# Large matmuls dealt out between small ones in attention; an evacuation moved ahead in the feed-forward

## The chip, the cores and the metric

One Trainium2 chip, one of its cores. The metric is the device time of one execution in microseconds; lower is better. Engines: PE (TensorE, matmuls and weight loads), DVE (VectorE), ACT (ScalarE), POOL (GpSimd) and SP, whose queue issues the DMAs.

## The reference

The kernel is one transformer layer on x of shape (2, 4096, 512), in fp32, with adaptive layer norms:

```
mod = silu(c) @ wmod                      # six rows: sa, ca, ga, sb, cb, gb
h   = layernorm(x) * (1 + ca) + sa
x   = x + ga * attention(h)               # RWKV-6, 16 heads of 32
h   = layernorm(x) * (1 + cb) + sb
x   = x + gb * ffn(h)

attention: xxx = h + sx * maa_x           # sx: the token before, minus this one
  m = tanh(xxx @ tm_w1); mix = maa + m @ tm_w2     # five mixes
  xw, xk, xv, xr, xg = h + sx * mix[i]
  r, k, v = xr @ Wr, xk @ Wk, xv @ Wv;  g = silu(xg @ Wg)
  w = exp(-exp(decay + tanh(xw @ td_w1) @ td_w2))
  per token: a = k v';  y = r (state + u a);  state = w state + a
  out = (groupnorm(y) * g) @ Wo
ffn: hh = silu(q(x) @ q(w_gate).T) * (q(x) @ q(w_up).T);  out = q(hh) @ q(w_down).T
  q: blocks of 16 along the last axis, rounded to FP4 (E2M1) values times the block's scale
```

The inner width of the feed-forward is 1408.

## The kernel before

**Order.** Nothing schedules the work at run time. Each engine runs a hand-written list of calls; counters (semaphores) tie the engines together, and `after(engine, signal, chunk, k)` makes an engine wait. An engine executes strictly in its own order, so a wait holds everything behind it.

**Attention** runs over 32 chunks of 128 tokens, both batches together. It is a pipeline over three chunks: body i prepares chunk i (`do_p`: mixes and projections), runs the recurrence of chunk c = i - 1 (`do_w`) and finishes chunk f = i - 2 (`do_f`: the product with Wo and the residual). Bodies 3 to 29 are a hardware loop whose lap holds nine bodies; the others are written out. All three parts are there in bodies 2 to 31.

The recurrence of a chunk is cut into eight steps n = 0 to 7: two batches by four blocks of 32 tokens. The parts of step n are, by engine:
- PE `pe_scores` (L424): products of 32x32 tiles of k and r, four row groups by four head slices, in three sets (L434, L438, L440).
- PE `pe_outer` (L442, matmuls L449): the outer products k v'. Its end signals `score_done`.
- DVE `dve_A` (L908): waits for `score_done`, builds the 32x32 decay-weighted matrix A in eight small instructions (its start is L919, s_tmp L926, masked copies L932) and updates the state (L948). Its end signals `A_done`.
- PE `pe_y` (L452; L464, L467): A times v plus state times r; needs `A_done` of its step. In PE's list y(n - 1) comes in step n. `pe_scores(n)` needs `A_done` of step n - 2.

All these small products are 192 matmul records in a step, each with a weight load. Between them stand the large products of the other chunks, each as a block:
- `pe_g` (L534, matmuls L543), the gate projection, one 128-column part in each of steps 0 to 3: four contraction steps k into the PSUM bank `SMALL`. `act_gu` on ACT reads the bank after parts 1 and 3.
- `pe_td1` (L505, L511) in step 4: the decay's first product, into `SMALL`; ACT's tanh (`u1_done`) reads it.
- `pe_wo` (L548, matmuls L558): the output product of chunk f, batch b, four contraction steps of 512 columns each into `SMALL`: b = 0 as (0, 1) in step 5 and (2, 3) in step 6, b = 1 whole in step 7. The first step of b = 0 needs `u1_done`, the first of b = 1 needs DVE's `dve_out(f, 0)` (L978, instruction L981), which reads the bank.
- `pe_td2` (L518) in step 6: the decay's second product, needs all five mixes; DVE's `dve_ww` (L822, L827) reads it.
- `pe_delta` (L498) at the end of steps 1 to 5, for `dve_mix` (L807; L814, and for the first mix L819). POOL adds hT to the other four mixes (`mixadd`, L764).

After step 7's y(6) come `pe_proj` (L530) for k's first half (needs `dve_ww`), y(7), the transposes `pe_x`, the other projections, `pe_tm1`, and scores(0) of the next chunk. On ACT `act_hT` (L613) turns the transposes into hT, on which DVE's `dve_sx` (L795) waits.

DVE's list in a body (`dve_body`, L983): A(0), z, A(1), mix 0, A(2), mix 1, layer-norm statistics, A(3), mix 2, A(4), mix 3, g, A(5), mix 4, A(6), ww, out(b = 0), A(7), out(b = 1), then the decay products (L836 on), yS (L955), sx (L795) and what follows.

**The feed-forward** runs over 64 tiles of 128 tokens, alternating between the two batches (u = 0, 1). For tile n, PE computes gate and up (L1623) in three column slices of 480, 464 and 464, in that order, for which four PSUM banks in two pairs are used in turn: slice 2 of a tile needs the pair of slice 0, so it waits for `dve_h(n, 0)`. Then PE runs the down product of tile n - 1 (L1632). ACT: sil of slice 0 (L1597), the grid and scales of the next tile's x (L1586, L1447), sil 1, statistics of the tile after (L1571 to L1577), sil 2, the layer norm, and the grid and full scales of h (`act_full`, L1447). DVE, in `dve_body` (L1519): the quantiser for x of tile n + 1 (`divide` and `quantise`, L1411 to L1439), `dve_h` for slices 1 and 2 of tile n (L1502), the quantiser for h of tile n (`dve_hq`, L1504), `dve_h` for slice 0 of tile n + 1, and `dve_out` (L1515) for tile n - 1. In the quantiser L1434 makes the rounded values q16h, and L1437 and L1439 multiply them by the high and low part of the scales, which gives hq; SP then issues two transposing DMAs (L1464, L1467) for the down product, behind them the store of the output and the load of a later tile (xl, L1473).

Of the kernel before, what the change touches and what calls it, by code (L numbers as in the profile page):

```python
# [160 lines left out]
def attention(nc, x1, x, maa_x, maa, tm_w1, tm_w2, decay, td_w1, td_w2, faaaa, Wr, Wk, Wv, Wg, Wo,  # L161
              ln_w, ln_b, c_in, wmod, ident_in, diag_in, pick_in, w_gate, w_up, early, ni=NI):
    with ExitStack() as ctx:
# [260 lines left out]
        def pe_scores(pe, c, n):  # L424
            b, q = divmod(n, Q)
            sc, scm = SC[n % 2], XB[n % 2]
            if n == 0:
                settled_after(pe, mod_done, (der, c), (ru_done, c), (m1_done, c), (k_done, c), (derk, c, 2))
            elif n >= 2:
                settled_after(pe, mod_done, (A_done, c, n - 1))  # L430
            for g in range(G):
                X = (g * B + b) * Q + q
                for d in HEADS:
                    nc.tensor.matmul(sc[d, g * NS:(g + 1) * NS], kvar[d, 0, g, b, 32 * q:32 * q + 32], rcol[d, X, 0:M1], start=True, stop=True)  # L434
            for g in range(G):
# [16 lines left out]
        def pe_y(pe, c, n):  # L452
            b, q = divmod(n, Q)
            if n == 0:
# [5 lines left out]
            for g in range(G):  # L460
# [7 lines left out]
            last.then_inc(y_done.sem, 1)  # L468
# [36 lines left out]
        def pe_td1(pe, i):  # L505
            xf_wait(pe, i, 0)
            after(pe, mf_done, i)
            after(pe, gu_done, i - 1)
            for k in range(G):
                for b in range(B):  # L510
                    last = nc.tensor.matmul(SMALL[HALVES[b], 0:TC], w_td1[:, k, :], xf[:, 0, k, b], start=(k == 0), stop=(k == G - 1))  # L511
            last.then_inc(td1_done.sem, 1)
# [21 lines left out]
        def pe_g(pe, c, g, do_p):  # L534
            if g == 0:
# [6 lines left out]
            for k in range(G):  # L542
                last = nc.tensor.matmul(SMALL[:, (g % 2) * BT:(g % 2 + 1) * BT], w_g[:, k, g * P:(g + 1) * P],  # L543
                                        xf[:, NMIX - 1, k].rearrange("p b t -> p (b t)"), start=(k == 0), stop=(k == G - 1))
            if g % 2:
                last.then_inc(proj_done.sem, 1)
# [15 lines left out]
        def pe_body(pe, i, do_p, do_w, do_f, more, more2):  # L562
            c, f = i - 1, i - 2
            if do_w:
                pe_g(pe, c, 0, do_p)
                pe_outer(pe, c, 0)
            for n in range(1, 8):
                if do_w:
                    pe_scores(pe, c, n)
                    pe_outer(pe, c, n)  # L570
                    if n <= 3:
                        pe_g(pe, c, n, do_p)
                if n == 4 and do_p:
                    pe_td1(pe, i)
                if n == 5 and do_f:
                    pe_wo(pe, f, 0, (0, 1), do_p, do_w)
                if n == 6 and do_f:
                    pe_wo(pe, f, 0, (2, 3), do_p, do_w)
                if n == 6 and do_p:
                    pe_td2(pe, i)  # L580
                if n == 7 and do_f:
                    pe_wo(pe, f, 1, (0, 1, 2, 3), do_p, do_w)
                if do_w:
                    pe_y(pe, c, n - 1)
                if n <= 5 and do_p:
                    pe_delta(pe, i, n - 1)
            if do_p:
                pe_proj(pe, i, 1, lambda h: after(pe, ww_done, i), (0,))
            if do_w:
                pe_y(pe, c, 7)  # L590
# [7 lines left out]
            if do_p:  # L598
                pe_proj(pe, i, 3, lambda h: after(pe, ru_done, i, h + 1))
                pe_scores(pe, i, 0)  # L600
# [382 lines left out]
        def dve_body(dve, i, do_p, do_w, do_f, more, more2):  # L983
            c, f = i - 1, i - 2
            for n in range(8):
# [14 lines left out]
                if n == 6 and do_f:  # L1000
                    dve_out(dve, f, 0)
# [82 lines left out]
def feed_forward(nc, out, x1, w_down, c_in, wmod, ident_in, early, nt=2 * NI):  # L1084
# [7 lines left out]
    with ExitStack() as ctx:  # L1092
# [326 lines left out]
        def quantise(dve, n, w, src, m, q, s, s16, s_done, full, full_done, pw, step, grid_done, dst, high, low, freed):  # L1419
# [14 lines left out]
            link(V.scalar_tensor_tensor(q[:], m, GRID, src, ALU.max, ALU.subtract))  # L1434
            freed()
# [68 lines left out]
        def dve_hq(dve, u, n):  # L1504
# [3 lines left out]
                     lambda: (after(dve, hT_high, n - 1), after(dve, hT_low, n - 1)))  # L1508
# [10 lines left out]
        def dve_body(dve, j, u, n, do_m, do_out, more):  # L1519
# [216 lines left out]
```

## Time and profile before

| | us |
|---|---|
| median of 3 runs | 4145.38 |
| lowest and highest | 4139.29, 4150.52 |
| the profiled execution | 4149.2 |
| its span in the profile | 4147.4 |
| one body of attention shown below | 72.8 |
| two successive feed-forward tiles | 22.06, 22.52 |

The span is the profile's time from the first to the last instruction; what lies around it is 1.8 us. Busy time of an engine is the time in which it had an instruction under way. For each instruction the profile says how long its engine was idle before it and what released it; "issue" means that it waited for nothing the profile shows. PE's matmuls overlap, so a group's time is from the start of the first to the end of the last. A matmul on fp32 data is two records.

### The profile page before, as it was taken

The numbers are of one execution on the slowest core, as the hardware profiler recorded it, in microseconds if no ns is written. First come the engines' busy times: TensorE is split into PE (matmuls) and PEld (weight loads), VectorE is DVE, ScalarE is ACT, GpSimd is POOL, SyncE is SP. The second block draws the span as 40 slices with busy tenths as digits, with TensorE's granted clock in tenths as the row PEclk, the third lists the DMA queues.
The fourth block names the chain that finished last, engine by engine and source line by source line (L and its number), as shares of the span: only waits on it lengthen the run. The fifth ranks groups of instructions, "written<-read, shape, count | busy, mean of one in ns | idle before, by whom it ended". The sixth has DMA issues, their size and how long they took to land. (4 is left out here: it accounts for less than half of the span.)

```text
span 4147.4 us, 151943 instructions
## 1 busy us (share of the span) xinstructions
PE 3600.3 (87%) x64072; PEld 2405.7 (58%) x64072; DVE 3358.0 (81%) x7542; ACT 1735.4 (42%) x3493; POOL 918.9 (22%) x737
## 2 busy tenths in 40 slices
PE   4889899898888888888988984299999999999998
PEld 3777677676676676776776762144444444444443
DVE  4788788887888877788887867878888888888887
ACT  2434444344344343443443412344444444444443
POOL 1122222221222222122221213522222222222221
PEclk7999999999999999999999986599999999999999
DMA  4000010000000000000000012023323323323322
GB/s 118 13 24 29 19 34 18 24 28 19 24 28 20 32 19 24 29 19 24 28 24 29 13 69 75 5 69 77 87 74 82 84 72 86 81 75 86 79 77 73
DMA packets 325485, 195.99 MB, mean 47 GB/s; under 512 B 265152, under 2 KB 265920, under 8 KB 324800
## 3 DMA queue, kind: packets, MB, share of 16 engines
q1 hardware_dynamic: 324800, 186.07, 16.2%
q8 instruction: 525, 8.60, 0.9%
q14 instruction: 160, 1.31, 0.1%
HBM read 89.56 MB, written 33.55 MB: 30 GB/s over the span
## 5 line engine op out<-in xcount | busy, mean ns | idle before, releaser
L932 DVE COPY_PREDICATED Am<-pick,banks 128x64 f32<-128x64 uint8 (+2 forms) x1792 | 461.2, 257 | 127.6 <-DVE Am L932 12.4
L764 POOL TENSOR_TENSOR raw_up<-raw_up,raw_gate 128x1024 f32<-128x1024 f32 x128 | 312.4, 2440 | 1084.9 <-DVE raw_up L814 1084.9
L1623 PE MATMUL fbank<-gT,xqT 128*128 128x464 f16 (+1 forms) x2304 | 491.4, 363 | 68.9 <-DVE h L1502 45.9
L1623 PE MATMUL fbank<-uT,xqT 128*128 128x464 f16 (+1 forms) x2304 | 487.7, 361 | 1.8 <-issue 1.7
L1632 PE MATMUL fbank<-dT,hqT 128*128 128x512 f16 x2112 | 467.8, 380 | 8.0 <-DMA hqT<-hq 8.0
L530 PE MATMUL banks<-raw_up,raw_gate 128*128 128x256 f32 x2048 | 459.0, 383 | 1.8 <-DVE xxx L827 1.8
L530 PEld LDWEIGHTS banks<-raw_up,raw_gate 128*128 128x128 f32 x2048 | 386.7, 191 | 54.2 <-issue 2.1
L1623 PEld LDWEIGHTS fbank<-gT,xqT 128*128 128x128 f16 x2304 | 221.2, 98 | 320.0 <-DVE h L1502 70.7
L1623 PEld LDWEIGHTS fbank<-uT,xqT 128*128 128x128 f16 x2304 | 225.4, 98 | 233.5 <-issue 3.1
L775 POOL TENSOR_TENSOR yrs<-yvar,neg_half 128x32 f32<-128x32 f32 x32 | 174.0, 5437 | 834.3 <-DVE yvar L961 834.3
L1632 PEld LDWEIGHTS fbank<-dT,hqT 128*128 128x128 f16 x2112 | 207.1, 98 | 255.9 <-DMA hqT<-hq 8.5
L558 PE MATMUL banks<-w_o,yn 128*128 128x512 f32 x512 | 275.0, 674 | 20.0 <-DVE yn L972 16.2
L814 DVE SCALAR_TENSOR_TENSOR raw_up<-banks,col_maa,sx 128x256 f32<-128x256 f32 x640 | 265.4, 477 | 29.4 <-PE banks L498 28.5
L543 PE MATMUL banks<-raw_up,w_g 128*128 128x256 f32 x1024 | 268.5, 406 | 19.1 <-issue 18.9
L634 ACT ACTIVATE m_stack<-xxx 32x256 fp32r<-32x256 f32 x512 | 211.9, 414 | 99.4 <-DVE xxx L805 80.9
L440 PE MATMUL banks<-rcol,kvar 32*32 32x16 f32 x8192 | 194.7, 177 | 60.5 <-issue 60.4
L438 PE MATMUL banks<-rcol,kvar 32*32 32x48 f32 x8192 | 204.5, 205 | 41.4 <-issue 41.1
L464 PEld LDWEIGHTS banks<-Am,v_s 32*32 32x32 f32 x8192 | 155.6, 107 | 145.3 <-issue 141.3
L530 PE MATMUL banks<-raw_up,w_v 128*128 128x256 f32 x1024 | 229.5, 382 | 0.0
L665 ACT ACTIVATE xxx<-xxx 128x1024 f32<-128x1024 f32 x32 | 33.8, 1057 | 466.6 <-DVE xxx L827 466.6
L543 PEld LDWEIGHTS banks<-raw_up,w_g 128*128 128x128 f32 x1024 | 191.3, 197 | 48.4 <-issue 21.4
L464 PE MATMUL banks<-Am,v_s 32*32 32x32 f32 x8192 | 190.0, 198 | 33.6 <-issue 32.6
(234 smaller groups left out, 7204.5 us busy)
## 6 DMA issues: line engine op xcount, KB each, us to landing
raw_scale<-in_L_attn_x SPq DMA_DIRECT2D x32, 512.0 KB, 3.7
xres<-in_L_attn_x SPq DMA_DIRECT2D x32, 512.0 KB, 3.7
x_after_attention<-xres SPq DMA_DIRECT2D x32, 512.0 KB, 3.4
xl<-x_after_attention SPq DMA_DIRECT2D x64, 256.0 KB, 2.7
xr<-x_after_attention SPq DMA_DIRECT2D x64, 256.0 KB, 2.7
out<-xr SPq DMA_DIRECT2D x64, 256.0 KB, 2.1
raw_gate<-in_L_ffn_w_gate SPq DMA_DIRECT2D x1, 2816.0 KB, 11.3
raw_up<-in_L_ffn_w_up SPq DMA_DIRECT2D x1, 2816.0 KB, 18.5
```

The costliest lines, as they stand in the source:

```text
L438: nc.tensor.matmul(scm[d, g * NM:g * NM + X0 - M1], kvar[d, 1, g, b, 32 * q:32 * q + 32], rcol[d, X, M1:X0], start=True, stop=True)
L440: nc.tensor.matmul(scm[d, g * NM + X0 - M1:(g + 1) * NM], kvar[d, 2, g, b, 32 * q:32 * q + 32], rcol[d, X, X0:SEND], start=True, stop=True)
L464: nc.tensor.matmul(out, v_s[d, g, b, q, :], Am[d, n % 2, g, :], start=True, stop=False)
L530: last = nc.tensor.matmul(PROJ[h][:, (g % 2) * BT:(g % 2 + 1) * BT], w[:, k, g * P:(g + 1) * P], buf[:, k].rearrange("p b t -> p (b t)"), ...
L543: last = nc.tensor.matmul(SMALL[:, (g % 2) * BT:(g % 2 + 1) * BT], w_g[:, k, g * P:(g + 1) * P], xf[:, NMIX - 1, k].rearrange("p b t -> p ...
L558: last = nc.tensor.matmul(SMALL[:], yn[:, k, b, :], w_o[:, b, k, :], start=(k == 0), stop=(k == G - 1))
L634: last = nc.scalar.activation(m_stack[rows, j, :], m_part[part % 2][HEADS[f], 0, :], ACT.Copy)
L764: nc.gpsimd.tensor_tensor(xf[:, j % NXF].rearrange("p g b t -> p (g b) t"), xf[:, j % NXF].rearrange("p g b t -> p (g b) t"), hT[:, :, :, ...
L814: last = nc.vector.scalar_tensor_tensor(xf[:, j % NXF, g], PROJ[g // 2][:, (g % 2) * BT:(g % 2 + 1) * BT].rearrange("p (b t) -> p b t", b= ...
L932: nc.vector.copy_predicated(dst, mask, src).then_inc((done or A_step).sem, 1)
L1623: last = nc.tensor.matmul(GU[2 * pair + t][:, 0:w], xqT[:, u, a, g, :], W[:, b_, g, lo_:hi_], start=(k == 0), stop=(k == 3 * G - 1))
L1632: last = nc.tensor.matmul(DN[v][:], hqT[:, v, a, kk, :], dT[:, b_, kk, :], start=(first and kk == 0), stop=(end and kk == KF - 1))
```

## The change

In attention the four functions `pe_scores`, `pe_y`, `pe_td1` and `pe_g` get an argument that says which part to issue. In step n, `between(place)` is called at four places: 0 between the two halves of scores(n), 1 between scores and outer, 2 after outer, 3 between the two halves of y(n - 1). In steps 1 to 3 it issues pe_g's k = 0, then (1, 2), then 3, at places 0 to 2; in step 4 pe_td1 in the same way. pe_wo for b = 0 goes one k at a time to places 1 and 3 of step 5 and 0 and 2 of step 6; for b = 1 to places 0, 2 and 3 of step 7 and its last k behind y(6). pe_td2 moves from step 6 to place 1 of step 7. The three sets of scores are now issued row group by row group. On DVE out(b = 0) moves from behind A(6) and ww to behind A(5), ahead of mix 4.

In the feed-forward, `dve_h` for slice 0 of the next tile moves into `quantise` of h: behind q16h (L1434), ahead of both hq products.

```diff
-        def pe_scores(pe, c, n):
+        def pe_scores(pe, c, n, gs):
...
-            if n == 0:
+            if gs[0] > 0:
+                pass
+            elif n == 0:
...
-            for g in range(G):
+            for g in gs:
                 X = (g * B + b) * Q + q
                 for d in HEADS:
                     nc.tensor.matmul(sc[d, g * NS:(g + 1) * NS], kvar[d, 0, g, b, 32 * q:32 * q + 32], rcol[d, X, 0:M1], start=True, stop=True)
-            for g in range(G):
-                X = (g * B + b) * Q + q
                 for d in HEADS:
...
         def pe_body(pe, i, do_p, do_w, do_f, more, more2):
             c, f = i - 1, i - 2
             if do_w:
-                pe_g(pe, c, 0, do_p)
+                pe_g(pe, c, 0, (0, 1, 2, 3), do_p)
                 pe_outer(pe, c, 0)
             for n in range(1, 8):
+
+                def between(place):
+                    if do_w and n <= 3 and place < 3:
+                        pe_g(pe, c, n, ((0,), (1, 2), (3,))[place], do_p)
+                    if do_p and n == 4 and place < 3:
+                        pe_td1(pe, i, ((0,), (1, 2), (3,))[place])
+                    if do_f and (n, place) in ((5, 1), (5, 3), (6, 0), (6, 2)):
+                        pe_wo(pe, f, 0, (((5, 1), (5, 3), (6, 0), (6, 2)).index((n, place)),), do_p, do_w)
+                    if do_p and n == 7 and place == 1:
+                        pe_td2(pe, i)
+                    if do_f and n == 7 and place != 1:
+                        pe_wo(pe, f, 1, ((0, None, 1, 2)[place],), do_p, do_w)
                 if do_w:
-                    pe_scores(pe, c, n)
+                    pe_scores(pe, c, n, (0, 1))
+                between(0)
+                if do_w:
+                    pe_scores(pe, c, n, (2, 3))
+                between(1)
+                if do_w:
                     pe_outer(pe, c, n)
-                    if n <= 3:
-                        pe_g(pe, c, n, do_p)
-                if n == 4 and do_p:
-                    pe_td1(pe, i)
-                if n == 5 and do_f:
-                    pe_wo(pe, f, 0, (0, 1), do_p, do_w)
-                if n == 6 and do_f:
-                    pe_wo(pe, f, 0, (2, 3), do_p, do_w)
-                if n == 6 and do_p:
-                    pe_td2(pe, i)
-                if n == 7 and do_f:
-                    pe_wo(pe, f, 1, (0, 1, 2, 3), do_p, do_w)
+                between(2)
                 if do_w:
-                    pe_y(pe, c, n - 1)
+                    pe_y(pe, c, n - 1, (0, 1))
+                between(3)
+                if do_w:
+                    pe_y(pe, c, n - 1, (2, 3))
                 if n <= 5 and do_p:
                     pe_delta(pe, i, n - 1)
+                if n == 7 and do_f:
+                    pe_wo(pe, f, 1, (3,), do_p, do_w)
...
+                if n == 5 and do_f:
+                    dve_out(dve, f, 0)
                 if 1 <= n <= 5 and do_p:
                     dve_mix(dve, i, n - 1)
...
-                if n == 6 and do_f:
-                    dve_out(dve, f, 0)
...
             link(V.scalar_tensor_tensor(q[:], m, GRID, src, ALU.max, ALU.subtract))
+            if meanwhile:
+                meanwhile()
             freed()
...
-                dve_hq(dve, u, n)
-            if more:
-                dve_h(dve, 1 - u, n + 1, 0)
+                dve_hq(dve, u, n, more)
```

## Rows read from the trace of the kernel before

**Rows 1.** The page: span, busy time by engine, and the instruction queue.

```profile
span 4147.4 us, 151943 instructions
...
PE 3600.3 (87%) x64072; PEld 2405.7 (58%) x64072; DVE 3358.0 (81%) x7542; ACT 1735.4 (42%) x3493; POOL 918.9 (22%) x737
...
q8 instruction: 525, 8.60, 0.9%
```

**Rows 2.** Windows, feed-forward: us, busy (instructions) by engine, PE clock, DMA share, GB/s.

```profile
3200.00:3600.00 400.00, 386.75 (x1885) 182.75 (x1882) 350.39 (x682) 186.14 (x288) 87.53 (x126) 1.00 0.32 79
```

**Rows 3.** Windows, one body of attention: steps to the first projection, then projections.

```profile
1393.80:1440.17 46.37, 37.83 (x1485) 28.98 (x1477) 40.47 (x118) 16.67 (x39) 10.68 (x6) 1.00 0.05 16
1440.17:1466.58 26.41, 26.41 (x309) 22.72 (x305) 20.74 (x39) 14.97 (x37) 5.44 (x1) 1.00 0.12 41
```

**Rows 4.** DVE's waits, 150 to 2480 us: us in total, times, longest.

```profile
DVE Am L919 <- PE banks L449: 92.8, 65, 7.6
...
DVE xres L981 <- PE banks L558: 31.0, 30, 2.7
```

**Rows 5.** PE's timeline, steps 5 to 7: start us, length, instruction, idle before.

```profile
1424.47 0.23 PE L464 MATMUL banks<-Am,v_s 32*32 32x32 f32 x5 [1.95 <-issue]
...
1428.10 0.21 PE L440 MATMUL banks<-rcol,kvar 32*32 32x16 f32 x3 [1.28 <-issue]
...
1428.47 0.46 PE L449 MATMUL banks<-v_s,kT 32*32 32x32 f32 x30
1428.86 1.98 PE L558 MATMUL banks<-w_o,yn 128*128 128x512 f32 x4
1430.77 1.16 PE L518 MATMUL banks<-u,raw_up 64*128 64x128 f32 x16
...
1435.46 0.44 PE L449 MATMUL banks<-v_s,kT 32*32 32x32 f32 x28 [1.59 <-issue]
1435.83 3.70 PE L558 MATMUL banks<-w_o,yn 128*128 128x512 f32 x8
...
1440.17 3.70 PE L530 MATMUL banks<-raw_up,raw_gate 128*128 128x256 f32 x16
```

**Rows 6.** Windows from the end of one stall to the next, and one DMA burst.

```profile
1419.00:1424.46 5.46, 3.51 (x127) 2.19 (x128) 5.36 (x11) 0.00 (x0) 3.53 (x2) 1.00 0.28 99
1424.46:1428.09 3.63, 2.35 (x126) 2.09 (x127) 3.12 (x12) 0.00 (x0) 0.27 (x1) 1.00 0.02 5
...
1428.09:1435.45 7.36, 5.77 (x254) 4.25 (x254) 6.65 (x17) 0.43 (x1) 2.17 (x1) 1.00 0.02 4
...
1425.50:1425.75 0.25, 0.25 (x4) 0.17 (x2) 0.19 (x1) 0.00 (x0) 0.00 (x0) 1.00 0.30 66
```

**Rows 7.** Two lines of the kernel: ns of one, min/median/max.

```profile
L449 PE MATMUL banks<-v_s,kT x7974: 184/191/258, 155.5 to 2479.6; 32*32 32x32 f32 x200
...
L926 DVE TENSOR_TENSOR s_tmp<-state,T x256: 270/283/2273, 128.5 to 2489.5; 128x128 f32<-128x128 f32 x128
```

**Rows 8.** DVE's timeline in the same body.

```profile
1427.12 1.66 DVE L814 SCALAR_TENSOR_TENSOR raw_up<-banks,col_maa,sx 128x256 f32<-128x256 f32 x4
...
1429.18 1.99 DVE L926 TENSOR_TENSOR s_tmp<-state,T 128x128 f32<-128x128 f32 x1
...
1448.45 1.23 DVE L795 TENSOR_TENSOR sx<-raw_gate 128x1024 f32<-128x1024 f32 x1 [1.98 <-ACT raw_gate L613]
```

**Rows 9.** Timelines of DVE, ACT and PE in one feed-forward tile.

```profile
3218.33 0.89 DVE L1437 TENSOR_TENSOR hq<-q16h,full_h 128x1408 f16<-128x1408 f16 x1 [0.29 <-DVE q16h L1434]
...
3229.88 0.70 DVE L1502 SCALAR_TENSOR_TENSOR h<-fbank,und,sil 128x464 f32<-128x464 f32 x1 [1.38 <-ACT sil L1597]
...
3217.44 0.64 ACT L1597 ACTIVATE sil<-fbank,und 128x480 f32<-128x480 f32 x1
...
3225.61 1.15 ACT L1447 ACTIVATE full_x<-s16x 128x512 f16<-128x512 f16 x2 [0.89 <-DVE s16x L1431]
...
3220.72 2.52 PE L1623 MATMUL fbank<-gT,xqT 128*128 128x464 f16 x12 [0.51 <-DVE h L1502]
```

More of the change, by code:

```diff
@@ L450, in pe_outer, with pe_y @@
             last.then_inc(score_done.sem, 1)
-        def pe_y(pe, c, n):
+        def pe_y(pe, c, n, gs):
             b, q = divmod(n, Q)
-            if n == 0:
+            if gs[0] > 0:
+                pass
+            elif n == 0:
                 settled_after(pe, mod_done, (A_done, c, n + 1), (yT_done, c - 1))
@@ L459, in pe_y @@
                 settled_after(pe, mod_done, (A_done, c, n + 1))
-            for g in range(G):
+            for g in gs:
                 X = (g * B + b) * Q + q
@@ L467, in pe_y @@
                     last = nc.tensor.matmul(out, state[d, b, q, g, :], r32[d, X, :], start=False, stop=True)
-            last.then_inc(y_done.sem, 1)
+            if gs[-1] == G - 1:
+                last.then_inc(y_done.sem, 1)
         def pe_x(pe, i):
@@ L503, in xf_wait, with pe_td1 @@
             after(eng, xf_done_v, i) if j == 0 else after(eng, xf_done_p, i, j)
[L505 to L509, printed above, removed]
+        def pe_td1(pe, i, ks):
+            if ks[0] == 0:
+                xf_wait(pe, i, 0)
+                after(pe, mf_done, i)
+                after(pe, gu_done, i - 1)
+            for k in ks:
                 for b in range(B):
                     last = nc.tensor.matmul(SMALL[HALVES[b], 0:TC], w_td1[:, k, :], xf[:, 0, k, b], start=(k == 0), stop=(k == G - 1))
-            last.then_inc(td1_done.sem, 1)
+            if ks[-1] == G - 1:
+                last.then_inc(td1_done.sem, 1)
         def pe_td2(pe, i):
@@ L532, in pe_proj, with pe_g @@
                 last.then_inc(proj_done.sem, 1)
-        def pe_g(pe, c, g, do_p):
-            if g == 0:
+        def pe_g(pe, c, g, ks, do_p):
+            if ks[0] > 0:
+                pass
+            elif g == 0:
                 xf_wait(pe, c, NMIX - 1)
@@ L541, in pe_g @@
                 after(pe, gu_done, c, 1)
-            for k in range(G):
+            for k in ks:
                 last = nc.tensor.matmul(SMALL[:, (g % 2) * BT:(g % 2 + 1) * BT], w_g[:, k, g * P:(g + 1) * P],
                                         xf[:, NMIX - 1, k].rearrange("p b t -> p (b t)"), start=(k == 0), stop=(k == G - 1))
-            if g % 2:
+            if g % 2 and ks[-1] == G - 1:
                 last.then_inc(proj_done.sem, 1)
@@ L589, in pe_body @@
             if do_w:
-                pe_y(pe, c, 7)
+                pe_y(pe, c, 7, (0, 1, 2, 3))
             if more:
@@ L599, in pe_body @@
                 pe_proj(pe, i, 3, lambda h: after(pe, ru_done, i, h + 1))
-                pe_scores(pe, i, 0)
+                pe_scores(pe, i, 0, (0, 1, 2, 3))
         def act_hT(act, i):
@@ L1417, in divide, with quantise @@
             assert k[0] == Q_SCALED
-        def quantise(dve, n, w, src, m, q, s, s16, s_done, full, full_done, pw, step, grid_done, dst, high, low, freed):
+        def quantise(dve, n, w, src, m, q, s, s16, s_done, full, full_done, pw, step, grid_done, dst, high, low, freed, meanwhile=None):
             blocks, bc, k, link = chain(dve, n, w, step, Q_SCALED)
@@ L1502, in dve_h, with dve_hq @@
             nc.vector.scalar_tensor_tensor(h[:, u, lo_:hi_], GU[2 * pair + 1][:, 0:w], und[:, u, 1:2], sil[:, pair, 0:w], ALU.mult, ALU.mult).then_inc(h_done.sem, 1)
-        def dve_hq(dve, u, n):
+        def dve_hq(dve, u, n, more):
             after(dve, h_done, n)
@@ L1507, in dve_hq @@
             quantise(dve, n, I_FF, h[:, u], mh[:], q16h, sh, s16h, hs_done, full_h, hfull_done, hp[:, u], hstep, hgrid_done, hq, hq_done, hlow_done,
-                     lambda: (after(dve, hT_high, n - 1), after(dve, hT_low, n - 1)))
+                     lambda: (after(dve, hT_high, n - 1), after(dve, hT_low, n - 1)),
+                     lambda: dve_h(dve, 1 - u, n + 1, 0) if more else None)
         def dve_out(dve, j, u, n):
```

## The prediction

> **What bounds the kernel now.** The page comes first [rows 1]: nothing is busy all the time (PE 87%, DVE 81%), so the average names no bound and the two halves have to be read apart. In the feed-forward's steady state PE is busy 386.8 and DVE 350.4 of 400 us [rows 2]; attention alternates inside one lap, so a window has to cover a whole lap of it.
>
> I took one body of attention's loop, one 128-token chunk in its pipelined form, from its first pe_g to the next one [rows 3]. It has two parts. In the part with the eight pe_scores/pe_outer/pe_y steps (46.4 us) PE is busy 37.8 us, so it stands idle 8.5 us. In the projections after it (26.4 us) PE is busy throughout. So whatever brings the first projection forward shortens the body; what PE idles in the steps is all that can be won. DVE's waits [rows 4] say how much it feels of this: 92.8 us for pe_outer and 31.0 us for pe_wo in 2330 us, about 4 us in each of 31 bodies.
>
> What is PE idle for? The timeline of steps 5 to 7 [rows 5] calls it "issue", with no releaser: 1.95, 1.28 and 1.59 us. Two things in the windows [rows 6] identify it. From the end of one stall to the end of the next there are 126 matmuls and 127 weight loads (3.63 us), and in the 7.36 us to the third stall 254 and 254: always about 254 instructions. And a short DMA burst (66 GB/s in 0.25 us, 16.5 KB) comes 1 us after a stall ends and 2.5 us before the next ends. The page's instruction queue moved 8.60 MB in 525 pieces, 16.4 KB each. So PE gets its instructions in pieces of about 256, asks for the next when it enters the last, and has it some 3.65 us later: each piece costs the larger of 3.65 us and the work in it. Thirty of pe_outer's 32x32 matmuls start within 0.27 us (0.46 less the length of one, 0.19 [rows 5, 7]), so small ones alone run through a piece in 1.2 us; a large product uses few instructions for much time. While DMA carried 99 GB/s of data one piece took 5.46 us.
>
> The Trainium skill ("Runtime: NRT & Kernel Launch", Instruction fetch mechanics) has the 16 KB pieces too, but says that the fetch is hidden by a slow issue and that PE's buffer holds 2048 instructions. With that, large products would cover nothing wherever they stand, and the attention part of this change would come to zero or less. The sum would then be the feed-forward's 2 us alone, 4143 us, against the 4113 below. The measured 254-instruction rhythm speaks against it.
>
> **Attention, part by part.** The same instructions are issued, so the number of pieces stays. What changes is which piece holds which large product.
>
> (a) pe_g, pe_td1 and the first pe_wo are cut up and put between halves of scores and y. A piece that holds a whole 2 us block beside 1.2 us or more of small work and a pe_delta comes near or over 3.65 us, while its neighbour ended in a stall of 1.3 to 1.9 us. In the body shown this imbalance is small: 7.36 us for two pieces is 3.68 each, so the lower bound is 0. The upper bound is one stall as it stands behind the first pe_wo block, 1.95 us. Where the pieces' borders fall shifts from body to body. I take 1.1 us a body, the middle, since blocks of 2 us meet a border in some bodies and miss it in others.
>
> (b) The last pe_wo (b = 1) stands unhidden before the projections: 3.70 us, from 1435.83 to 1439.5, after the last stall [rows 5]. Its first quarter (0.95 us) now goes between the halves of scores(7), ahead of that stall: a gain of 0.95 less an added switch. But pe_td2 (1.1 us) moves from before y(5) to after scores(7), so where the border falls in scores(7) it has left the covered side for the uncovered one: a loss of 1.1 plus switches, 1.3 us. Shown body: gain 0.75. A body does not hold a whole number of pieces, so the border wanders evenly over 128 matmuls from body to body, and the two kinds come about equally often. (0.75 - 1.3) / 2 is a loss of 0.3; some cases lie between, so I take a loss of 0.1.
>
> (c) Switches between small and large. The last matmul of outer(6) starts about 1428.74 (1428.47 + 0.46 less 0.19), pe_wo at 1428.86: 0.12 us where small ones follow at 0.01. With the way back I take 0.2 us per insertion. There are some 13 more in a body, 2.6 us of PE time. Most fall into pieces that end in a stall of over 1 us and cost nothing; were all of that cover gone they would cost 2.6 us. One (in y(6)) is uncovered and is in (b).
>
> (d) outer(n) now comes up to 1.5 us of large product later after scores(n), and DVE's A(n) waits for it. In the stall rhythm its place is set by the piece, not by the work before it. I take 0; bounds 0 and 1.5 us in a few steps.
>
> (e) dve_out(f, 0) moves from behind A(6) and dve_ww to behind A(5), ahead of dve_mix(4). Before, A(5) ends at 1427.1 (mix starts 1427.12) and the second pe_wo block only at 1430.8 [rows 5, 8]. The last quarter now ends about 0.95 us earlier, near 1429.8. So DVE will stand at dve_out for 2.7 us in every body. Queued behind it are dve_mix(4) (1.66 us), A(6), dve_ww and A(7); PE's td2 waits for mix(4), y(6) for A(6), the first projection for ww, and POOL's last mixadd for mix(4). In PE's order, from the last quarter: y(5) 0.6, half scores 0.6, wo quarter 0.95, half scores 0.6, td2 1.1, outer 0.4, quarter 0.95 = 5.2 us until y(6). On DVE: out 0.7, mix 1.6, A(6) 2.7 = 5.0 us until y(6) is free. Just level. That counts A(6) at its undisturbed length: in the shown body its second instruction took 1.99 us against a median of 0.28 [rows 7, 8], while POOL ran its mixadd. After the change outer(6) is finished long before, so A(6) follows mix(4) at once and gets ahead of POOL; if not, 1.7 us are added and DVE leads. At the end of the steps DVE is some 1.8 us further behind PE than now; it has 1.98 us of wait for hT to take that up [rows 8]. I take 0.
>
> Sum: 1.1 - 0.1 = 1.0 us in each of the 30 bodies with all parts: -30 us. Bounds per body: -2.2 to +1.5 us.
>
> **Feed-forward.** dve_h(n+1, 0) moves from behind both hq products to ahead of them. The rows of one tile [rows 9]: PE stood 0.51 us at slice 2 for this h, so it looks as if PE would gain that. But who sets the 22 us period? DVE's only long gap is 1.38 us ahead of its third h, and its releaser is ACT's sil, which comes late because ACT has first waited for DVE's own s16x and then runs its statistics. DVE and ACT drive each other in a ring that PE is not in. So PE's 0.51 us goes to another wait of PE. In the ring the move does two things. It covers the 0.29 us between q16h and hq, which stands in every second tile: 31 x 0.29 = 9 us. And h now needs ACT's sil, which ends at 3218.08 (3217.44 + 0.64), just when q16h ends (3218.33 - 0.29 = 3218.04): about 0.07 us of new wait in each of 62 tiles, 4 us. hq is 0.5 us later for the transposes, behind which SP has the out store and the next xl load; what slack that load has these rows do not show. Its bounds are 0 and the 0.3 us of delay left by a 0.29 us shorter ring, in 62 tiles, 19 us; I take 3, as ACT's own chain shows no wait for it here. Sum -9 + 4 + 3 = -2 us; bounds -9 and +14.
>
> Together -32 us. The profiled run took 4149.2 us for a span of 4147.4 us; the median of the three runs shown is 4145.4. The span should come to 4115, the median to 4113 us. Differences under 0.3% (12 us) are not told from none.
>
> **Rivals.**
> - Forecast: uneven pieces get even, 0.4 to 1.8 us a body, -14 to -56 us: 4089 to 4131. Chance 0.48.
> - The smoothing is worth more: nearly every stall behind a large block goes and A(6)'s 1.7 us with it, 2.2 us a body, 30 bodies -66: about 4078. For it: the 8.5 us idle in [rows 3]. Against it: most of that is the 3.65 us floor itself. 0.15.
> - Nothing: PE is at the rate of its instruction supply, and that rate does not care where large products stand. Only the end effects stay, -0.2 to +0.3 us a body: 4140 to 4152. For it: 3.63, 3.68 and 3.68 us per piece in the shown body. The skill's rule would lead here by another way. 0.20.
> - Slower: the early dve_out makes DVE the bound. If the wo quarters end no earlier than 1430.8 (3.7 us after A(5)) and A(6) keeps its 1.99 us collision, DVE needs 0.7 + 1.6 + 4.4 = 6.7 us to y(6) against PE's 5.2: +1.5 us a body, +45 us: 4190. It decides from the point at which DVE needs more than PE's 5.2 us plus the piece's stall there. 0.11.
> - PE bounds the feed-forward after all: 0.51 us in 62 tiles, -32 us on top of the forecast: 4082. Against it: the ring above. 0.06.
>
> The likeliest gives 4113; its own range is 4089 to 4131. For 8 in 10: 4072 to 4150, which leaves the slower rival and the far end of the second out. Faster than 0.3%: the forecast (0.46 of it), the large smoothing, the feed-forward rival: 0.67. Same: the third rival and the edge of the first: 0.20. Slower: 0.13.
>
> **What would show it.** In the profile after: the same 254-instruction rhythm; fewer or shorter "issue" stalls in the steps, PE idle there near 7.5 us instead of 8.5; DVE waits for pe_wo (now at dve_out ahead of mix 4) up from 31 to about 80 us, its waits for pe_outer down; no 2 us s_tmp in A(6). The projection part unchanged at 26.4 us. In the feed-forward: no PE wait at slice 2, DVE's 1.38 us wait for sil unchanged, the 0.29 us gap gone, the period still 22.1 to 22.5 us. Wrong it would be if the body did not shorten though stalls shrink (then switches or DVE ate it), if A(6) still collided with POOL, or if the feed-forward period moved by over 0.3 us.

## The result: attention shorter, feed-forward as before

The changed kernel takes 4100.19 us (median of 4 runs, 4095.98 to 4103.1), the kernel before 4147.95 us on the same chip (4139.29 to 4151.67). The ratio is 0.9882, 95% interval [0.9862, 0.9903]: faster by 1.2%. I had predicted 4113 us against 4145, a ratio of 0.992. The sign and the place were right and the size fell short. The gain is all attention's. From the first to the last yS transpose (32 of them, so 31 bodies) before takes 2317.4 us and after 2274.0; from the first to the last `tmpo` of the feed-forward (64) before takes 1391.6 us and after 1390.4.

The page of after, whose lines answer to [rows 1]:

```profile
span 4100.9 us, 151913 instructions
...
PE 3687.1 (90%) x64072; PEld 2390.0 (58%) x64072; DVE 3323.2 (81%) x7542; ACT 1736.3 (42%) x3493; POOL 922.8 (23%) x737
```

The kernel is 46.5 us shorter in span and PE is busy 86.8 us more. So the change made PE's work dearer and took away more idle time than it added work. The same in windows, whose columns are those of [rows 3]: from the first yS transpose to the last, before,

```profile
177.50:2494.90 2317.40, 2044.10 (x55059) 1626.21 (x55057) 1850.56 (x4749) 959.93 (x2270) 488.77 (x209) 0.97 0.08 26
```

and after; the other two lines are one body, steps and projections, as in [rows 3]:

```profile
176.00:2450.00 2274.00, 2123.36 (x55059) 1616.12 (x55057) 1818.39 (x4748) 960.00 (x2270) 491.69 (x209) 0.98 0.08 26
...
1368.23:1414.12 45.89, 41.43 (x1489) 29.20 (x1478) 39.36 (x116) 15.62 (x38) 10.71 (x6) 1.00 0.06 16
1414.12:1440.41 26.29, 26.29 (x305) 22.60 (x304) 21.61 (x41) 16.02 (x38) 5.44 (x1) 1.00 0.12 41
```

PE idled 273.3 us in before's stretch and idles 150.6 us in after's; in the body shown 4.5 us where [rows 3] have 8.5. The projections are as they were. PE's timeline of steps 5 to 7 after the change, against [rows 5]:

```profile
1398.33 0.23 PE L466 MATMUL banks<-Am,v_s 32*32 32x32 f32 x4 [1.06 <-issue]
...
1403.16 0.47 PE L449 MATMUL banks<-v_s,kT 32*32 32x32 f32 x32
1403.57 1.13 PE L565 MATMUL banks<-w_o,yn 128*128 128x512 f32 x2
...
1406.21 0.21 PE L466 MATMUL banks<-Am,v_s 32*32 32x32 f32 x2 [0.93 <-issue]
...
1408.80 1.16 PE L523 MATMUL banks<-u,raw_up 64*128 64x128 f32 x16
...
1413.15 1.13 PE L565 MATMUL banks<-w_o,yn 128*128 128x512 f32 x2
1414.12 1.24 PE L535 MATMUL banks<-raw_up,raw_gate 128*128 128x256 f32 x5
```

The block of 3.70 us directly ahead of the projections is gone; one quarter stands there. But in this body that isn't yet a gain: the last stall ends at 1406.21, ahead of scores(7), so pe_td2 and all four quarters of pe_wo(b=1) come behind it, and PE works without a pause up to the first projection:

```profile
1406.21:1414.12 7.91, 7.91 (x228) 4.86 (x228) 6.35 (x25) 2.28 (x3) 2.35 (x1) 1.00 0.02 5
```

In [rows 5] 4.71 us lie between the last stall and the first projection. The instruction rhythm of [rows 6] is still there; windows from stall to stall, one piece and two:

```profile
1394.46:1398.32 3.86, 2.80 (x126) 1.93 (x127) 3.45 (x12) 0.31 (x1) 0.22 (x1) 1.00 0.54 137
1398.32:1406.20 7.88, 6.95 (x254) 4.29 (x254) 6.30 (x15) 0.00 (x0) 2.87 (x1) 1.00 0.02 6
```

DVE's waits in attention, 150 to 2440 us, against [rows 4]:

```profile
DVE xres L999 <- PE banks L565: 96.1, 34, 5.9
...
DVE Am L937 <- PE banks L449: 60.8, 36, 7.1
```

DVE now stands 96.1 us at dve_out (31.0 before) and 60.8 us for pe_outer (92.8). And in step 6 A(6) no longer meets POOL's mixadd ([rows 8]: 1.99 us):

```profile
1404.73 0.69 DVE L999 TENSOR_TENSOR xres<-banks,xres 128x512 f32<-128x512 f32 x1 [1.06 <-PE banks L565]
1405.34 1.65 DVE L832 SCALAR_TENSOR_TENSOR raw_up<-banks,col_maa,sx 128x256 f32<-128x256 f32 x4
...
1407.10 0.28 DVE L944 TENSOR_TENSOR s_tmp<-state,T 128x128 f32<-128x128 f32 x1
...
1422.32 1.23 DVE L813 TENSOR_TENSOR sx<-raw_gate 128x1024 f32<-128x1024 f32 x1 [1.17 <-ACT raw_gate L631]
```

**What my prediction did not look at: the clock.** PE's granted clock in the attention stretch is 0.97 before and 0.98 after. Cut into windows of 1 us, it is full except in short stretches at 0.50, the 1.2 GHz level. One of them, in before:

```profile
1120.00:1121.00 1.00, 0.69 (x49) 0.55 (x37) 1.00 (x4) 0.78 (x2) 0.00 (x0) 1.00 0.00 0
1121.00:1122.00 1.00, 0.00 (x0) 0.00 (x0) 1.00 (x3) 0.00 (x0) 0.17 (x1) 1.00 0.37 53
1122.00:1123.00 1.00, 0.97 (x76) 0.93 (x77) 0.91 (x2) 0.00 (x0) 1.00 (x1) 1.00 0.85 248
1123.00:1124.00 1.00, 1.00 (x2) 0.49 (x3) 1.00 (x2) 0.00 (x0) 1.00 (x1) 0.50 0.66 240
...
1126.00:1127.00 1.00, 1.00 (x63) 0.55 (x64) 0.89 (x4) 0.00 (x0) 0.00 (x0) 0.79 0.00 0
```

and PE's timeline there:

```profile
1122.03 0.23 PE L438 MATMUL banks<-rcol,kvar 32*32 32x48 f32 x2 [1.35 <-issue]
...
1122.86 3.67 PE L558 MATMUL banks<-w_o,yn 128*128 128x512 f32 x4
```

PE had stood 1.35 us for its next piece of instructions; 1 us later the clock fell, and the half of pe_wo that takes 1.98 us in [rows 5] took 3.67. This fall cost 1.7 us of PE's time; some last longer, and the mean is 1.9 us. There are 32 stretches with falls in before's 31 bodies and 15 in after's. Each of them begins in, or shortly behind, a stall of 1.2 to 5.8 us. The reverse does not hold: before has 90 stalls over 1.3 us there and after 25, so most stalls are followed by no fall.

That gives a book for each profile, which adds up by the way it is made: the stretch from the first yS to the last is PE's work at full clock, plus what the lower clock added (busy time times one less the granted clock, summed over 1 us windows), plus idle time. All in us, from one profile each; the last column is the ratio to before from the timed runs. The variants were timed in three groups, each beside its own runs of the kernel before (medians 4140.88, 4140.48 and 4152.42 us), so they are compared with the change by their ratios; a ratio is the record's own and can differ from the quotient of the two medians by 0.2%. Before, e0 and e1 have the same attention but for the order inside pe_scores, after and e2 have the same.

| kernel | stretch | work | clock | idle | ratio [95%] |
|---|---|---|---|---|---|
| before | 2317.4 | 1982.3 | 61.8 | 273.3 | |
| e0_none | 2312.8 | 1984.7 | 58.9 | 269.1 | 0.9986 [0.9969, 1.0002] |
| e1_ffn_only | 2304.0 | 1982.6 | 64.1 | 257.3 | 1.0006 [0.9990, 1.0021] |
| after | 2274.0 | 2092.9 | 30.5 | 150.6 | 0.9882 [0.9862, 0.9903] |
| e2_attention_only | 2260.9 | 2093.7 | 23.0 | 144.1 | 0.9893 [0.9873, 0.9912] |
| e3_late_out | 2289.7 | 2080.0 | 36.4 | 173.3 | 0.9975 [0.9958, 0.9992] |
| e4_g_td1_only | 2280.7 | 2051.0 | 34.4 | 195.3 | 0.9954 [0.9936, 0.9972] |
| e5_wo_td2_out_only | 2278.3 | 2020.5 | 47.0 | 210.8 | 0.9953 [0.9929, 0.9976] |
| e6_out_moved_only | 2399.2 | 1978.3 | 98.7 | 322.2 | 1.0228 [1.0207, 1.0248] |
| e7_after_less_g | 2252.6 | 1995.6 | 43.6 | 213.4 | 0.9886 [0.9863, 0.9909] |
| e8_before_less_g | 2281.8 | 1898.2 | 79.0 | 304.6 | 0.9935 [0.9913, 0.9957] |
| e9_after_less_small | 2135.1 | 2020.1 | 19.8 | 95.2 | 0.9563 [0.9540, 0.9586] |
| e10_two_cuts | 2284.7 | 2059.7 | 52.9 | 172.1 | 0.9912 [0.9889, 0.9935] |
| e11_wo1_earlier | 2261.8 | 2085.2 | 35.3 | 141.3 | 0.9857 [0.9836, 0.9879] |

Stretches of the same attention differ by up to 13 us between profiles, so the means are compared: 2311.4 = 1983.2 + 61.6 + 266.6 for the three at the top, 2267.5 = 2093.3 + 26.8 + 147.4 for after and e2. Per body of 31: work +3.55, clock -1.12, idle -3.85 us, together -1.42. Over the variants the clock's column follows the idle time: 20 us at 95 us of idle time (e9), 99 us at 322 (e6).

### The profile page after: what moved, and what is told of

It reads as the page before. It is cut to its first block and busy times, and to the rows that moved or that the text cites. A ratio compares the mean times of both kernels' runs of the same rounds, so it can differ in the third digit from the quotient of the medians.

```text
span 4100.9 us, 151913 instructions
## 1 busy us (share of the span) xinstructions
PE 3687.1 (90%) x64072; PEld 2390.0 (58%) x64072; DVE 3323.2 (81%) x7542; ACT 1736.3 (42%) x3493; POOL 922.8 (23%) x737
## 5 line engine op out<-in xcount | busy, mean ns | idle before, releaser
L1642 PE MATMUL fbank<-gT,xqT 128*128 128x464 f16 (+1 forms) x2304 | 490.1, 363 | 56.4 <-DVE h L1522 30.5
L436 PE MATMUL banks<-rcol,kvar 32*32 32x80 f32 x8192 | 337.8, 237 | 26.4 <-issue 25.9
L550 PE MATMUL banks<-raw_up,w_g 128*128 128x256 f32 x1024 | 310.3, 415 | 9.7 <-issue 9.4
L565 PE MATMUL banks<-w_o,yn 128*128 128x512 f32 x512 | 298.5, 667 | 20.8 <-DVE yn L990 16.2
L438 PE MATMUL banks<-rcol,kvar 32*32 32x48 f32 x8192 | 292.7, 204 | 20.8 <-issue 20.7
L440 PE MATMUL banks<-rcol,kvar 32*32 32x16 f32 x8192 | 255.1, 178 | 26.7 <-issue 26.2
L436 PEld LDWEIGHTS banks<-rcol,kvar 32*32 32x32 f32 x8192 | 175.8, 107 | 153.7 <-issue 133.9
L438 PEld LDWEIGHTS banks<-rcol,kvar 32*32 32x32 f32 x8192 | 217.8, 107 | 22.3 <-issue 22.2
```

Of the source, the lines that this page charges most:

```text
L565: last = nc.tensor.matmul(SMALL[:], yn[:, k, b, :], w_o[:, b, k, :], start=(k == 0), stop=(k == G - 1))
L1642: last = nc.tensor.matmul(GU[2 * pair + t][:, 0:w], xqT[:, u, a, g, :], W[:, b_, g, lo_:hi_], start=(k == 0), stop=(k == 3 * G - 1))
```

## Experiments

**The two halves.** e1 has only the feed-forward's edit, e2 only attention's. e1, the core of its edit:

```diff
             link(V.scalar_tensor_tensor(q[:], m, GRID, src, ALU.max, ALU.subtract))
+            if meanwhile:
+                meanwhile()      # dve_h(dve, 1 - u, n + 1, 0)
             freed()
```

> Attention as before, only the feed-forward's dve_h moved. My theory (DVE and ACT drive each other in a ring, PE is not in it): -2 us, inside -9 to +14, so no difference that can be told; PE's wait for h shrinks and turns up elsewhere. Rival (PE bounds the feed-forward): about -32 us.

4138.92 us against 4140.88, ratio 1.0006: no difference. My -2 us can't be told from that, and the rival (PE bounds the feed-forward, -32 us) is out.

e2 is the change with that edit undone:

```diff
-                     lambda: (after(dve, hT_high, n - 1), after(dve, hT_low, n - 1)),
-                     lambda: dve_h(dve, 1 - u, n + 1, 0) if more else None)
+                     lambda: (after(dve, hT_high, n - 1), after(dve, hT_low, n - 1)))
...
+            if more:
+                dve_h(dve, 1 - u, n + 1, 0)
```

> Only the attention part of the change. My theory: it is all of the gain, -43 to -48 us, as the two spans from the first to the last yS differ by 43.3 us (2317.4 and 2274.1). Rival (the feed-forward gives a good part of it): -15 us or so.

4093.45 us, ratio 0.9893: the whole gain, within the intervals.

**The two parts of attention.** Both have the feed-forward's edit, and their diffs are against the change. e4 deals out pe_g and pe_td1 and leaves the rest in blocks and dve_out late; e5 is its complement.

```diff
                     if do_p and n == 4 and place < 3:
                         pe_td1(pe, i, ((0,), (1, 2), (3,))[place])
-                    if do_f and (n, place) in ((5, 1), (5, 3), (6, 0), (6, 2)):
-                        pe_wo(pe, f, 0, (((5, 1), (5, 3), (6, 0), (6, 2)).index((n, place)),), do_p, do_w)
-                    if do_p and n == 7 and place == 1:
-                        pe_td2(pe, i)
-                    if do_f and n == 7 and place != 1:
-                        pe_wo(pe, f, 1, ((0, None, 1, 2)[place],), do_p, do_w)
+                    if place == 2 and n == 5 and do_f:
+                        pe_wo(pe, f, 0, (0, 1), do_p, do_w)
+                    if place == 2 and n == 6 and do_f:
+                        pe_wo(pe, f, 0, (2, 3), do_p, do_w)
+                    if place == 2 and n == 6 and do_p:
+                        pe_td2(pe, i)
+                    if place == 2 and n == 7 and do_f:
+                        pe_wo(pe, f, 1, (0, 1, 2, 3), do_p, do_w)
```

> Attention only as far as pe_g (steps 1 to 3) and pe_td1 (step 4) are cut up; pe_wo, pe_td2 and dve_out as before; the feed-forward as after. If the gain is that large products cover the wait for instructions wherever they are dealt out, these 24 cuts' share is about half, -15 to -30 us. Rival (the early steps are paced by DVE or by the supply itself, and only the end of the steps, with pe_wo, counts): 0 to -8 us.

4115.23 us, ratio 0.9954: -19 us, as expected. The core of e5's edit:

```diff
-                    if do_w and n <= 3 and place < 3:
-                        pe_g(pe, c, n, ((0,), (1, 2), (3,))[place], do_p)
-                    if do_p and n == 4 and place < 3:
-                        pe_td1(pe, i, ((0,), (1, 2), (3,))[place])
+                    if do_w and n <= 3 and place == 2:
+                        pe_g(pe, c, n, (0, 1, 2, 3), do_p)
+                    if do_p and n == 4 and place == 2:
+                        pe_td1(pe, i, (0, 1, 2, 3))
```

> The other half of the attention part: pe_wo dealt out, pe_td2 moved to step 7, dve_out(b = 0) ahead of mix 4; pe_g and pe_td1 stay blocks; the feed-forward as after. Smoothing everywhere: -15 to -30 us. Rival (only the end of the steps counts): -38 to -48 us, nearly all. If DVE's 96 us of waits at dve_out were on the path, it would be slower than before by up to 45 us.

4116.63 us, ratio 0.9953: -19 us, as expected, and not nearly all of the gain. The two halves add up to e2's 44 us within the intervals. The book shows the same trade in both: work +68 and +37 us over the mean of before, idle -71 and -56, clock -27 and -15. e5 holds three edits (pe_wo dealt out, pe_td2 later, dve_out earlier), which it doesn't part.

**A control.** e0 undoes all but the order inside pe_scores (the small products of one g behind one another, not all first ones ahead).

> The control: all blocks, pe_td2 and dve_out as before, the feed-forward as before; left of the change is only that the three sets of scores are issued row group by row group. My theory (same instructions, same supply): no difference, 4135 to 4147 us. Rival (the order inside the scores is part of the gain that the variant with pe_g and pe_td1 cut up showed): -10 to -20 us.

4144.24 us against 4152.42, ratio 0.9986 [0.9969, 1.0002]: no difference that can be told. So the gain isn't one of that order.

**The end of the steps.** e3 keeps everything dealt out, but has td2 back in step 6, pe_wo(b=1) as two quarters behind outer(7), one in y(6) and one behind it, and dve_out late:

```diff
-                    if do_p and n == 7 and place == 1:
+                    if do_p and n == 6 and place == 2:
                         pe_td2(pe, i)
-                    if do_f and n == 7 and place != 1:
-                        pe_wo(pe, f, 1, ((0, None, 1, 2)[place],), do_p, do_w)
+                    if do_f and n == 7 and place in (2, 3):
+                        pe_wo(pe, f, 1, ((0, 1), (2,))[place - 2], do_p, do_w)
...
-                if n == 5 and do_f:
-                    dve_out(dve, f, 0)
...
+                if n == 6 and do_f:
+                    dve_out(dve, f, 0)
```

> The change without its reordering at the end of the steps: pe_g, pe_td1 and pe_wo (b = 0) dealt out as in the change, but pe_td2 stays in step 6, dve_out(b = 0) stays behind A(6) and ww, and pe_wo (b = 1) stays behind outer(7), cut as (0, 1), 2, 3. My theory (term b: the early quarter and the late td2 about cancel): within 0.3% of the change, 4085 to 4110 us. Rival (the early dve_out and the quarter ahead of the last stall are what the second half of the gain is): 4110 to 4120 us.

4130.25 us against 4140.48, ratio 0.9975: about a fifth of the change's gain. My expectation fell, and the time is past the rival's 4110 to 4120 us too: where these three stand at the end of the steps is worth 22 us in the profiled stretch (2289.7 less 2267.5) and 38 in the timed runs (0.9975 less 0.9882); the profiled execution was 10 us faster than the median. In the book e3's work is 13 us less than the change's, its idle time 26 us more and its clock loss 10 us more than the means of after and e2. So the loss is not large work that stands bare; it is stalls that nothing fills any more, and falls that follow them. Which of the three does it, this run doesn't say. One thing more: e3 is e4 with pe_wo dealt out as well, and gains no more than e4 (0.9975 [0.9958, 0.9992] against 0.9954 [0.9936, 0.9972]). Dealing out pe_wo without the other moves brought nothing, so the 19 us of e5 are not shown to come from the dealing alone.

**dve_out moved alone.** e6 is before with only that:

```diff
+                if n == 5 and do_f:
+                    dve_out(dve, f, 0)
                 if 1 <= n <= 5 and do_p:
                     dve_mix(dve, i, n - 1)
...
-                if n == 6 and do_f:
-                    dve_out(dve, f, 0)
```

> The kernel before with one edit: dve_out(b = 0) behind A(5), ahead of mix 4; PE's list unchanged. DVE then waits some 3.6 us a body for pe_wo, and pe_td2, next in PE's list, waits 2.3 us for mix 4. If DVE and PE are then in series: +1 to +2.3 us in 30 bodies, 4170 to 4210 us. Rival (PE's wait for mix 4 only takes the place of its wait for instructions, and the slack behind takes up the rest): under +12 us, about 4141 to 4150 us.

4233.36 us against 4140.48, ratio 1.0228: 93 us slower, 3 us a body. It went beyond what either theory had. The wait itself is as the first theory said. PE's waits, 150 to 2440 us:

```profile
PE banks L518 <- DVE raw_up L814: 71.7, 29, 2.5
```

In before this wait of pe_td2 for DVE's mix 4 does not exist. It is 2.5 us in 29 bodies and takes the place of some supply stalls, so idle time grows by only 56 us over the mean of before. The other 37 us are the clock: 48 stretches with falls, 98.7 us lost against 61.6. Windows over the same times of both, before and e6; the clock's column is the last but two:

```profile
1000.00:1700.00 700.00, 616.14 (x16236) 490.26 (x16235) 559.45 (x1420) 298.39 (x708) 150.68 (x64) 0.98 0.07 24
```

```profile
1000.00:1700.00 700.00, 607.54 (x15892) 483.38 (x15893) 536.85 (x1384) 282.46 (x671) 144.08 (x63) 0.95 0.07 24
```

**Is PE bound by its instructions?** If it is, large products in the steps are free and small ones are not. e7 is the change without two of the four large products of pe_g in steps 1 to 3 (the gate is then incomplete), e8 the same from before; both leave out about 3 us of PE work a body.

```diff
-                        pe_g(pe, c, n, ((0,), (1, 2), (3,))[place], do_p)
+                        pe_g(pe, c, n, ((0,), (), (3,))[place], do_p)
```

> The changed kernel, but pe_g leaves out k = 1 and 2 in steps 1 to 3, so the gate is not computed fully: 3.0 us of large products a body less, with only 48 of PE's 3580 instructions. If the steps are paced by the supply of instructions, the large products lie in its waits and little is gained: -10 to -30 us. Rival (PE's work is the bound): 3.0 us in 31 bodies, -93 us.

> The same products left out of the kernel before, where they stand in blocks of 2 us that become 1 us. Supply theory: a 1 us block fits into a piece as the dealt ones do, so this gains about what the dealing of pe_g did plus what is left out of e7: -25 to -45 us. Rival (work is the bound): -93 us here too.

e7: 4094.61 us, ratio 0.9886, the change's own 0.9882. 98 us of work less, and 66 us of them came back as idle time and 17 as clock loss; the 15 us left in the book don't show in the timed runs. That is less gain than the -10 to -30 us expected, and far from the rival's -93. (Three insertions a body are left out with the products, so the 98 us hold some switching too; e8's 85 us hold none.) PE's waits of e7, 150 to 2440 us, where after has 26.2 and 21.7 us for these two lines:

```profile
PE banks L440 <- issue: 97.4, 116, 1.7
PE banks L466 <- issue: 58.3, 72, 4.2
```

e8: 4115.3 us, ratio 0.9935, a gain of 27 us, within the -25 to -45 us expected, for 85 us of work left out; 38 came back as idle time and 17 through the clock. Even this kernel, with less to do, is slower than the change.

e9 takes the other side: the change without the third set of small score products in steps 1 to 7 (scores incomplete), 6950 matmuls fewer and about as many weight loads.

```diff
-                for d in HEADS:
+                for d in HEADS if n == 0 else ():
                     nc.tensor.matmul(scm[d, g * NM + X0 - M1:(g + 1) * NM]
```

> The changed kernel without the third set of scores (32x16 products) in steps 1 to 7, so part of A is wrong: 448 of PE's 3580 instructions a body, but only 7 x 0.2 = 1.4 us of its work. Supply theory: 1.75 pieces of 3.65 us = 6.4 us a body less supply time, of which DVE, then near its own limit of about 41 us for the steps, lets through 2 to 5 us: -60 to -150 us. Rival (work is the bound): at most 1.4 us in 31 bodies, -43 us.

3971.82 us, ratio 0.9563, 0.9677 of the change: -132 us, 4.3 us a body, for 73 us of PE work. Idle time falls by 52 us with it. And the supply lets go of PE in part: its "issue" waits between the first yS and the last fall from 147 us in after to 41, and it now waits 51 us for DVE. From 150 to 2440 us:

```profile
PE banks L466 <- DVE Am L950: 30.1, 35, 1.4
PE banks L501 <- DVE raw_up L832: 20.9, 27, 0.8
```

Two versions of the dealing. e10 makes two cuts of pe_g and pe_td1, not three, since switches cost work:

```diff
-                        pe_g(pe, c, n, ((0,), (1, 2), (3,))[place], do_p)
+                        if place != 1:
+                            pe_g(pe, c, n, ((0, 1), None, (2, 3))[place], do_p)
```

> The changed kernel with pe_g and pe_td1 cut in two instead of three: k = (0, 1) between the score halves, (2, 3) behind outer. Four switches less a body (0.2 us each), outer(n) 0.5 us earlier. If switches cost only where no stall covers them: within 8 us of the change. Rival (a switch always costs): -24 us from the change.

4114.08 us, ratio 0.9912. Work does fall, by 34 us, and 25 us come back as idle time and 26 through the clock. By the ratios it is 12 us slower than the change, where I had expected at most 8 us and the rival -24 us. The intervals overlap, so it may be no difference, but the rival is out: fewer switches did not make it faster.

e11 brings pe_wo(b=1)'s quarters forward, so that none stands directly ahead of the projections:

```diff
-                        pe_wo(pe, f, 1, ((0, None, 1, 2)[place],), do_p, do_w)
+                        pe_wo(pe, f, 1, ((0, 1), None, (2,), (3,))[place], do_p, do_w)
...
-                if n == 7 and do_f:
-                    pe_wo(pe, f, 1, (3,), do_p, do_w)
```

> The changed kernel with pe_wo (b = 1) one place earlier: k = (0, 1) between the halves of scores(7), 2 behind outer(7), 3 between the halves of y(6), nothing behind y(6). My theory (what goes ahead of the last stall is hidden): another 0.95 us in about half of the bodies plus one switch less, -10 to -20 us from the change. Rival (outer(7) comes 0.95 us later and DVE's A(7), now level with PE, with it): 0 to +15 us.

4098.04 us against 4152.42, ratio 0.9857 [0.9836, 0.9879]: the lowest of those that compute everything. It beats before; from the change (0.9882) it can't be told, though the 10 us between them are what was expected.

## Why the prediction was right, and where its terms were off

**The bound.** Right. Steps are paced by pieces of about 254 instructions (e7 and e9 above), the projections by PE's work. Between two stalls one piece apart a piece takes 3.4 us at least in both kernels, 3.9 to 4.0 in the median; the 3.65 us of the prediction are one body's.

**(a) and (c), the exchange of stalls for switches.** The mechanism is as told and both sides were too small. Idle time fell by 3.85 us a body and not by about 1, and the dearer work is 3.55 us a body and not 2.6. I had called that work hidden under stalls of over 1 us; it is hidden, but it also uses up what I would have booked as gain. Net, the two are -0.3 us a body. That the dealing makes pieces more even can be counted. With the steps cut every 254 PE instructions from stall to stall (some 360 pieces a trace), pieces with under 3 us of PE work are 38% in before and 28% in after, those with over 4 us 27% and 20%; before has 143 stalls over 1 us, after 48. In [rows 5]'s body the middle of 0 and 1.95 us would have been 0.98, not 1.1.

**The missing term.** The step that failed in size is the sum itself, "1.1 - 0.1 = 1.0 us": it knew only work and stalls. The clock takes 1.12 of the 1.42 us a body in the book, a term that the prediction put at nothing. How much of a fall reaches the end is less sure, since a slowed large product also fills time before the next piece. Bodies 2 to 29 without any fall take 73.2 us in before, e0 and e1 (24 of them) and 72.1 in after and e2 (34), all bodies 74.8 and 73.3. By that count 1.1 of 1.5 us are there without a fall. But those bodies are picked: they are the ones with short stalls. So by these two counts the clock's share lies between 0.4 and 1.1 us a body, and which it is stays open. If it is the larger, work and stalls alone gave 0.3 us a body, 9 us, and the forecast's range was hit by luck; if it is the smaller, the 1.0 us was right. e6 points to a real cost: its stretch grew by 88 us where idle time grew by 56 and work by nothing; but no run changes the clock alone. [Rows 3 and 6] show a body at 1.00, and I read no further; the column was in every window.

**(b), the quarter of pe_wo against td2.** Wrong: I took a loss of 0.1 us a body, of a gain of 0.75 and a loss of 1.3. The body shown above is one of the losing kind. e3 shows that the arrangement at the end is worth 22 to 38 us, 0.7 to 1.2 us a body; the border of the pieces does not decide it alone. Its split stays open.

**(e), dve_out ahead of mix 4.** DVE waits 96 us there (about 80 said), and the level chain held: PE has no wait for mix 4 in attention beyond 0.5 us at one line. I put that down to td2, which moved with it; that pe_wo's quarters end earlier must help too, and no run parts the two. In e6, with td2 left in place and pe_wo in blocks, DVE leads as in the slower rival, but at another place (PE waits at pe_td2 for mix 4, not at y(6)) and at twice its price (93 us against 45). A(6)'s collision with POOL is gone: after has no s_tmp over 0.6 us in step 6, before 15; in steps 4 and 5 they remain (36 against 39). What that alone is worth no run shows.

**(d)** Nothing shows against the 0 taken: DVE's waits for pe_outer fell.

**The rivals.** "Nothing, the supply does not care" is refuted (e4, with e0 beside it): the rate per piece is fixed, but a piece with 2 us of large work too many runs over it, and dealing makes such pieces rarer. The larger smoothing (4078) and the feed-forward rival (4082) did not come. The slower rival did not come in the change itself. The rule of the Trainium skill ("Runtime: NRT & Kernel Launch", Instruction fetch mechanics) that the fetch is hidden would have given 4143 us; e9 and e7 speak against it as the rhythm did.

**Feed-forward.** Period and total as said. After, one tile, against [rows 9], DVE:

```profile
3206.60 0.70 DVE L1522 SCALAR_TENSOR_TENSOR h<-fbank,und,sil 128x464 f32<-128x464 f32 x1 [1.37 <-ACT sil L1616]
...
3215.55 1.63 DVE L1452 SCALAR_TENSOR_TENSOR q16h<-mh,h 128x1408 f16<-128x1408 f32 x1
3217.32 0.72 DVE L1522 SCALAR_TENSOR_TENSOR h<-fbank,und,sil 128x480 f32<-128x480 f32 x1
3217.95 0.88 DVE L1457 TENSOR_TENSOR hq<-q16h,full_h 128x1408 f16<-128x1408 f16 x1
```

and PE:

```profile
3218.09 2.52 PE L1642 MATMUL fbank<-gT,xqT 128*128 128x464 f16 x12 [0.61 <-DVE h L1522]
3223.84 2.33 PE L1651 MATMUL fbank<-dT,hqT 128*128 128x512 f16 x10 [0.87 <-DMA hqT<-hq]
```

The 0.29 us gap is covered and sil's 1.37 us stands, as predicted. "No PE wait at slice 2" was wrong: it is 0.61 us here. Over all tiles (2740 to 4080 us) PE's waits for h fell from 41.7 to 27.9 us, and new ones came (4.9 us for hqT, 2.5 for xqT). As argued, PE's waits there partly move about, and e1 shows that shortening them gains nothing. That DVE and ACT set the period is argued from [rows 9], not tested.

## What to carry to other kernels

Where an engine runs many tiny instructions, look for a rhythm in its "issue" stalls before costing work: large instructions in such a stretch are nearly free as long as each piece has its share, and fewer small ones are worth more than their own time. Book every stretch as work at full clock, clock loss and idle time, with the granted clock read in windows of 1 us; a stall of 1.2 us or more can cost its length again when the clock falls behind it. When an instruction is moved forward in one engine's list, look at what stands behind it there and who waits for that: in e6 dve_out, moved ahead of mix 4, made PE's pe_td2 wait in every body.

## What the runs showed of the hardware that I had not expected

- The clock falls that follow some of the stalls, most of them of 1.3 to 2 us (rows above: 1.35 us of standing, then 0.50), 1.9 us each in the mean: 62 us of before's attention.
- Two bodies in every profile have one long stall ahead of pe_g's first product: 4.5 and 5.0 us in before (L543), 4.5 to 5.3 us in all fourteen profiles. In before these are the eleventh and the twentieth, which take 81.5 and 79.9 us where the mean is 74.8. They lie where the hardware loop goes back. The Trainium skill ("Runtime: NRT & Kernel Launch", Instruction fetch mechanics) says that a taken branch whose target lies outside the engine's present window of two pages forces a fetch ahead of execution; the place agrees, but no run here moved the branch, and the last body has stalls as long (5.2 and 4.7 us in before) with no branch back.
- Switching PE between 32x32 and full products costs work: 110 us in 31 bodies for some 13 more insertions a body, 0.27 us each (0.2 predicted from [rows 5]). The other dealings agree: 0.27 us with 8 more insertions (e4) and with 9 (e10), 0.28 with 11 (e3), 0.24 with 5 (e5).
